# Another order of work in three stages of a fused attention and feed-forward kernel: GpSimd in the experts, all engines in the latent attention, the last units of the feed-forward

## The reference

```python
x = x + grouped_attention(layernorm(x), ctx, ctx)   # 32 query heads, 8 heads of ctx, width 8
x = x + routed_experts(layernorm(x))                # top 2 of 8 experts and 4 identities, SiLU gate
x = x + latent_attention(layernorm(x), ctx)         # 16 heads, rotary queries and keys
x = x + mx_feed_forward(layernorm(x))               # 256 -> 1024 -> 256, SiLU gate
# latent attention, per head h:
q   = rope(x @ Wq[h].T @ w_kc_q[h]) @ W_qr[h]       # 128x256 -> 192 -> 64
k   = rope(ctx) @ W_kr[h]
p   = softmax(q @ k.T)
out = sum_h (p @ rope(ctx)) @ w_kc_kv[h].T @ Wo[:, h].T
# feed-forward: inputs and weights are quantised in blocks of 32 (shared power of two, few mantissa bits)
```

## Time and profile before

| | us |
|---|---|
| median of 3 runs (lowest, highest) | 818.46 (818.2, 818.87) |
| the profiled execution | 819.62 |
| its span, first to last instruction | 817.80 |
| busy in the span: TensorE / VectorE / GpSimd / ScalarE | 749.2 / 594.5 / 567.1 / 403.1 |
| mean granted clock of TensorE | 0.981 of full |

### The profile page before, as it was taken

The page is one execution under the profiler, slowest core; times in us unless marked ns, Lnnn a source line. Parts: engine busy times, 40 slices in busy tenths (PEclk is TensorE's granted clock), DMA queues, the critical chain, the costliest instruction groups (busy, mean ns, idle before and its releaser), DMA issues. The chain is left out here.

```text
span 817.8 us, 14830 instructions
## 1 busy us (share of the span) xinstructions
PE 749.2 (92%) x4801; PEld 538.7 (66%) x4808; DVE 594.5 (73%) x1087; ACT 403.1 (49%) x1068; POOL 567.1 (69%) x590
## 2 busy tenths in 40 slices
PE   3999999878999998789999999999999999876786
PEld 2555555457888887656877777777777777653464
DVE  5888889856777878656465575886678675749994
ACT  1688887532323323226455545545444545454463
POOL 5677776425867667465656878787887787817996
PEclk9999999979999999989999999999999999997999
DMA  9300000040100010322200000000000000000001
GB/s 249 122 2 0 0 0 1 1 171 1 39 20 19 19 58 0 107 76 70 84 15 1 1 1 2 2 1 1 1 1 1 2 1 1 1 2 7 26 34 39
DMA packets 8763, 24.12 MB, mean 29 GB/s; under 512 B 1711, under 2 KB 5167, under 8 KB 8087
## 3 DMA queue, kind: packets, MB, share of 16 engines
q1 hardware_dynamic: 8154, 23.28, 8.6%
q10 hardware_dynamic: 549, 0.08, 0.1%
HBM read 21.26 MB, written 2.10 MB: 29 GB/s over the span
## 5 line engine op out<-in xcount | busy, mean ns | idle before, releaser
L1622 POOL TENSOR_TENSOR q<-turned 64x512 f32<-64x512 f32 x128 | 168.0, 1312 | 25.7 <-DVE turned L1548 9.5
L1299 PE MATMUL ps<-l_yt,a 128*128 128x512 f32 x576 | 146.0, 404 | 2.1 <-ACT p L1445 1.7
L1299 PEld LDWEIGHTS ps<-l_yt,a 128*128 128x128 f32 x576 | 106.2, 190 | 27.8 <-issue 4.7
L1609 POOL TENSOR_TENSOR p<-p,l_inverse 128x512 f32<-128x512 f32 x64 | 66.9, 1047 | 74.7 <-DVE l_inverse L1570 74.3
L1445 ACT ACTIVATE p<-ps,l_negmax 128x128 f32<-128x128 f32 x256 | 91.1, 382 | 43.2 <-DVE l_negmax L1539 43.1
L1548 DVE TENSOR_TENSOR turned<-ps,rope 128x1024 f32<-128x1024 f32 x64 | 78.1, 1221 | 45.0 <-PE ps L1299 42.3
L881 PE MATMUL ps<-yt_experts,wsplit 128*128 (+1 forms) x384 | 97.1, 401 | 0.2 <-DVE inner L979 0.2
L467 DVE TENSOR_REDUCE negmax<-ps 128x4 f32<-128x512 f32 x128 | 85.2, 686 | 14.8 <-PE ps L290 13.4
L881 PEld LDWEIGHTS ps<-yt_experts,wsplit 128*128 128x128 f32 x384 | 71.1, 192 | 14.4 <-DVE inner L979 0.5
L1539 DVE TENSOR_REDUCE l_negmax<-ps 128x4 f32<-128x512 f32 x64 | 41.2, 686 | 44.3 <-PE ps L1357 44.1
L383 ACT ACTIVATE pt<-ps 128x512 f32<-128x512 f32 x128 | 69.9, 599 | 5.2 <-PE ps L312 3.5
(11 more groups left out here) (214 smaller groups left out, 1566.5 us busy)
## 6 DMA issues: line engine op xcount, KB each, us to landing
wide<-in_wide SPq DMA_DIRECT2D x8, 768.0 KB, 4.4
mx_raw<-in_mx SPq DMA_DIRECT2D x8, 384.0 KB, 3.1
x<-in_x SPq DMA_DIRECT2D x4, 512.0 KB, 9.1
ctx_t<-in_ctx_t SPq DMA_DIRECT2D x1, 2048.0 KB, 7.9
out<-x SPq DMA_DIRECT2D x16, 128.0 KB, 1.7
narrow<-in_narrow SPq DMA_DIRECT2D x8, 192.0 KB, 2.8
ktraw<-in_ctx_rows SPq DMA_DIRECT2D x1, 1248.0 KB
wraw<-in_gate SPq DMA_DIRECT2D x1, 1024.0 KB, 18.8
```

The lines of the kernel that those rows point to most:

```text
L1299: out = pe.matmul(tile_bank(n, k), a[i][:, pa, kin, k * 128:(k + 1) * 128], yt[j % 2][:, py, kin, :, :].rearrange("p b s -> p (b s)"), sta ...
L1609: pool.tensor_tensor(p[:, head, :, :], p[:, head, :, :], spread(inverse[:, head, :], 2, S), ALU.mult).then_inc(normed[head], 1)
L1622: t = pool.tensor_tensor(out[rows[(head + half) % 2], head, :], turned[rows[head], half, :], turned[rows[head], 2 + half, :], ALU.add)
```

## The change

Experts: in a step GpSimd now does `ht`, divide, rotate, scale, quantise (the quantising moves behind rotation and scaling), and `scale_x` moves from x = 6 and 7 to 5 and 6. The memset of the bound is one more step of the semaphore chain of the routes (21 becomes 22).

Latent attention: TensorE's list becomes tiles 0 and 1, spare 0, tile 2, narrow product of n-1, spare 1, context of n-3, scores of n-1, both heads' transposes of n-2, spare 2, both halves of the projection of n-3, spare 3. The narrow product's full matmul is split into two of 64 columns, one per head. The context moves to bank 1, p's transposes to another of the changing banks and to the bank of the narrow product, and the waits follow the banks. The places `spare` hold query weights half 0, context weights, query weights half 1, narrow weights; the next group's rows are transposed at places 0 and 2, front's result at 2. ScalarE's copy of the context moves behind `qs`, VectorE's low part of it behind the rotations, and front's pieces on VectorE move from the end of its list to between the maxima and the first rotation, at k = 3, 4, 6, 7, 8, 9 (`deviations` at 4). SyncE also waits for the query weights before it loads the next wide weights.

Feed-forward: the multiplication by the scale of unit 14, and of the second half of unit 15, move from GpSimd to VectorE, behind the clips, with a semaphore `late_made`.

```diff
@@ routed_experts, GpSimd
-                if x == 6:
+                if x == 5:
                     pool.tensor_tensor(group, group, run_of(factor[:, :, :], j).to_broadcast([S, 4, E]),
...
                 if inside(u - 3, UNITS):
                     pool.wait_ge(h_hi, u - 2)
                     pool.tensor_tensor(ht[old][:, 1, :], h[old][:, :], ht[old][:, 0, :].bitcast(F32),
                                        ALU.subtract).then_inc(h_lo, 1)
+                if inside(v, UNITS) and x % 2 == 0:
+                    divide(4 * jv + xv // 2, xv)
                 if inside(u, UNITS) and x < ROTARY_STEPS:
                     rotate_context(pool, m, rotated, j, x)
-                if inside(u, UNITS) and x in (6, 7):
+                if inside(u, UNITS) and x in (5, 6):
                     scale_x(j, x)
+                if inside(v, UNITS) and x % 2:
+                    quantise(4 * jv + xv // 2, xv)
@@ latent_attention
-        ctx_ps, rows_ps = q_ps, m.ps16[:, 1, :]
+        ctx_ps, rows_ps = m.bank(1), m.ps16[:, 1, :]
...
-        turned_p_bank = lambda n, head: (changing[n % 2], m.bank(3))[head]
+        turned_p_bank = lambda n, head: (changing[(n + 1) % 2], q_ps)[head]
@@ latent_attention, SyncE
                 wait(sp, c_made, i - 1)
+                wait(sp, a_made, 2 * (i - 1))
                 load_wide(sp, m, d, i)
@@ latent_attention, TensorE: narrow_product
-                    wait(pe, cs_lo, n - 1)
+                    wait(pe, p_kept[1], n - 1)
...
-                    pe.matmul(q_ps, b[i][:, 1, :], q[n % 2][:, 2, :], start=False, stop=True).then_inc(narrowed, 1)
+                    for head in range(2):
+                        t = pe.matmul(q_ps[rows[head], :], b[i][:, 1, head * CE:(head + 1) * CE], q[n % 2][:, 2, :],
+                                      start=False, stop=True)
+                    t.then_inc(narrowed, 1)
@@ latent_attention, TensorE: context
                     wait(pe, cs_lo, n)
+                    pe.wait_ge(tile_turned, min(TILES * (n + 3) + 2, TILES * STEPS))
@@ latent_attention, TensorE: the list of a step
                 tile(n, 2)
                 narrow_product(n - 1)
                 spare(n, 1)
+                context(n - 3)
+                score(n - 1)
                 turn_p(n - 2, 0)
+                turn_p(n - 2, 1)
+                spare(n, 2)
                 project(n - 3, 0)
-                turn_p(n - 2, 1)
                 project(n - 3, 1)
-                spare(n, 2)
-                score(n - 1)
-                context(n - 2)
                 spare(n, 3)
@@ latent_attention, ScalarE: the list of a step
                 exponential(n - 2, 0)
-                keep_context(n - 3)
                 exponential(n - 2, 1)
                 spare(n, 0)
                 keep_narrow(n - 1)
                 spare(n, 1)
+                keep_context(n - 3)
                 keep_p(n - 2, 0)
                 keep_p(n - 2, 1)
@@ latent_attention, VectorE: the list of a step
                 maximum(n - 2, 0)
                 maximum(n - 2, 1)
+                for k, part in ((3, f.add), (4, f.statistics), (6, f.scales), (7, f.divide), (8, f.clip), (9, f.multiply)):
+                    if front_in(n, k) is not None:
+                        part(dve, m, front_in(n, k))
                 rotate_both(n, 0)
                 invert(n - 2, 0)
-                split_context(n - 3)
                 rotate_both(n, 1)
                 invert(n - 2, 1)
                 spare(n, 0)
                 rotate_last(n)
                 spare(n, 1)
+                split_context(n - 3)
                 spare(n, 2)
...
-                for k, part in ((2, f.add), (3, f.statistics), (6, f.scales), (7, f.divide), (8, f.clip), (8, f.multiply)):
-                    if front_in(n, k) is not None:
-                        part(dve, m, front_in(n, k))
@@ feed_forward, VectorE
                 if n == B:
+                    scale_back(n - 2)
                     clip_halves()
+                    scale_back_half()
...
+            def scale_back(n):
+
+                wait(dve, hq_turned, n - 1)
+                dve.wait_ge(hc_made, n + 1)
+                dve.tensor_tensor(blocks(hq[n % 2][:, :]), blocks(hc[n % 2][:, :]), spread(hscale[n % 4][:, :], 2, MX),
+                                  ALU.mult).then_inc(late_made, 1)
+
+            def scale_back_half():
+
+                dve.wait_ge(hq_turned, B - 2)
+                dve.wait_ge(hc_made, B + 1)
+                dve.tensor_tensor(half_of(hq[1], 1), half_of(hc[1], 1), spread(hscale[(B - 1) % 4][:, 16:32], 2, MX),
+                                  ALU.mult).then_inc(late_made, 1)
```

More of the change, by code:

```diff
@@ L44 @@
 TOP_SCALE = 1.5
-ROUTE_STEPS, ROTARY_STEPS = 21, 5
+ROUTE_STEPS, ROTARY_STEPS = 22, 5
 HEADS, CQ, CQH, KDIM = 16, 192, 96, 128
@@ L1083, in step @@
                     pool.wait_ge(rotated, ROTARY_STEPS * j + x)
-                if inside(u, UNITS) and x == 7:
+                if inside(u, UNITS) and x == 6:
                     pool.wait_ge(affine, j + 4)
@@ L1276, in spare @@
                         pe.wait_ge(y_lo, 2 * j + 1)
-                    turn(j, place, w_ps)
-                if fj is not None and place == 0:
+                    turn(j, place // 2, w_ps)
+                if fj is not None and place == 2:
                     pe.wait_ge(y_lo, 2 * min(fj + 2, GROUPS - 1) + 2)
@@ L1423, in spare @@
                         keep_narrow_weights(i, w_ps)
-                if j is not None and place < 2:
-                    keep_rows(j, place, w_ps)
-                if fj is not None and place == 0:
+                if j is not None and place in (0, 2):
+                    keep_rows(j, place // 2, w_ps)
+                if fj is not None and place == 2:
                     f.keep(act, fj, rows_ps)
@@ L1518, in spare @@
                 if i is not None:
-                    if place < 2:
-                        split_queries_weights(i, place, w_ps)
-                    elif place == 2:
+                    if place in (0, 2):
+                        split_queries_weights(i, place // 2, w_ps)
+                    else:
                         split_context_weights(i, w_ps)
-                if j is not None and place < 2:
-                    split_rows(j, place, w_ps)
+                if j is not None and place in (0, 2):
+                    split_rows(j, place // 2, w_ps)
             def last_statistics():
@@ L2009, in body @@
                     wait(pool, hq_turned, n - 2)
-                    for half in range(2):
-                        pool.wait_ge(hc_made, B + half)
-                        pool.tensor_tensor(half_of(hq[1], half), half_of(hc[1], half),
-                                           spread(hscale[(place - 1) % 4][:, half * 16:(half + 1) * 16], 2, MX),
-                                           ALU.mult).then_inc(hq_made, 1)
-                elif inside(n - 1, B):
+                    pool.wait_ge(hc_made, B)
+                    pool.tensor_tensor(half_of(hq[1], 0), half_of(hc[1], 0), spread(hscale[(B - 1) % 4][:, 0:16], 2, MX),
+                                       ALU.mult).then_inc(hq_made, 1)
+                elif inside(n - 1, B - 2):
                     pool.wait_ge(hc_made, n)
```

73 lines of the change are left out of this document (40 added, 33 removed).

## The result

The changed kernel took 805.65 us (median of 4 runs, 802.32 to 809.57) beside 818.33 of the kernel before (4 runs, 817.68 to 818.87): ratio 0.9847, interval 0.9802 to 0.9892, that is 12.7 us less where 12.5 were forecast. Run again (experiment `after_again`), it took 807.14 beside 819.18: 0.9837, interval 0.9816 to 0.9858. So the sum came out. That it came out this near is in part luck: of its terms some were too large and some too small by 1 to 2 us, and these errors cancel; the part on why lists them.

What follows compares the result with a forecast made beforehand. TensorE bounds the latent attention, GpSimd and VectorE waits the feed-forward, GpSimd's `ht` the experts' holes. -9.1 - 1.5 - 1.4 + 4.0 - 3.8 - 0.7 = -12.5 us, from 818.46 to 806.0 us, range 800 to 814.5.

Steps and rivals of the forecast that it cites:

- the order in steps 7 to 30: Latent attention, TensorE: two fewer tile changes at 0.19 us save 0.38 a step, -9.1 us in all (-4.3 to -10.6).
- the waits: Latent attention: copies, normalisations, turned rows and front's pieces arriving late in the new step cost +4.0 us together.
- steps 3 to 6: Latent steps that also make the weights: they lose at least as many tile changes, -1.5 us.
- the tail: Last latent iterations: the last scores stand behind one context instead of two transpose and project blocks, -1.4 us (-2.4 to 0).
- steps 0 to 2: First three latent steps: they wait for VectorE's splits of the weights either way, 0 us (-1 to +4).
- the experts: GpSimd's rotation ahead of quantising closes three TensorE holes, -2.85 us; scalings one place earlier, -1.0; together -3.8.
- the feed-forward's end: Unit 14's multiplication and the last second half move from GpSimd to VectorE: -0.7 us, between -0.2 and -1.5.
- rival 2: Latent blocks: tile changes are not what makes them long, so the overheads stay; 816.6 us, chance 0.08.
- The normalisations: ScalarE's later work delays the third tile in steps 9, 13, 21 and 29 by 0.3 us each.
- rival 1: Latent steps: waits for `qs` (+5.6 us), or pieces on VectorE and ScalarE, eat most of the gain; 810 to 814.5, chance 0.22.
- rival 3: Narrow product: the second pair of halves doesn't run side by side, +30.7 us, 837 us; chance 0.05.
- Front's pieces: VectorE, ahead of the rotations: `scales` in steps 14, 22 and 30 delays them, +0.3 us each, +0.9; at worst +5.

Runs made afterwards that it cites:

- experts_only: The kernel before with the experts' part of the change alone: 816.83 us, ratio 0.9968.
- unsplit: The changed kernel with the narrow product's second part in one piece of 128 columns again, the order kept: 817.32 us, ratio to the kernel before 0.9973.
- turns_together: The kernel before with the second head's four transposes moved ahead of both halves of the projection, nothing else: 821.3 us, ratio 1.0036.
- front_late: The changed kernel with front's pieces on VectorE behind the last split of a step again, at their old steps: 815.14 us, ratio to the kernel before 0.9958.
- split_alone: The kernel before with only the narrow product's second part split into two halves, the order kept: 819.55 us, ratio 1.0003.
- scale_late: The changed kernel with GpSimd's two scalings of x back in steps 6 and 7 of a group: 806.06 us, ratio to the kernel before 0.9831.
- ff_only: The kernel before with the feed-forward end of the change alone: 817.61 us, ratio 0.9971.
- latent_only: The kernel before with the latent part of the change alone: 810.88 us, ratio 0.9884.

## Why the prediction was right, step by step

Against the forecast, the order in steps 7 to 30 saved 1.8 us more, the waits cost 1.2 less and steps 3 to 6 saved 0.5 more; the tail came out 1.5 worse, steps 0 to 2 0.7, the experts 0.3 and the feed-forward's end 0.2. Each is taken up below.

**The change of tile: its price right, the whole gain a little too small.** Forecast 0.38 a step, found 0.45 (10.873 - 10.420), in 24 steps 10.9 us instead of 9.1, 0.3 beyond the upper bound; against the 10.85 of `experts_only` it is 10.4. The two changes themselves are 0.36 (`unsplit`), 0.18 each where 0.19 was taken; rival 2 is out. The other 0.07 to 0.09 is there with five changes too: 0.02 to 0.04 of it comes with the transposes in one block (`turns_together`), and the rest may lie in which tiles meet; that was not isolated. The upper bound itself was added up wrongly: 0.27 + 0.17 are the shares of two blocks and not of two changes. With the projection's 0.08, which the working puts to the same change as the scores' 0.27, the two largest changes make 0.52, or 12.5 us. I also looked for the overhead mostly in the block behind the change. The first halves, 1.01 or 0.91 by what follows them, show that the block ahead of a change carries part of it. So the context, with no change ahead of it any more, did not fall under 0.95, as I had named for a sign, but only to 0.97; a change still stands behind it. The tiles, whose share I could not separate, gave 0.11. The Trainium skill (TensorEngine Tiling (Array Packing), "Key Properties") states that changing the tiling mode, not merely the tile, drains TensorE. These runs agree as far as they go: a change of mode takes 0.18 to 0.24 us here at full clock. That it is a drain, they do not show.

**The waits, forecast +4.0, found +2.8** (256.47 - 264.60 + 10.9). The rows of the next group: 1.16 above a plain step (1.23 in step 7) and 0.1 in the step behind it, before 0.88 (0.85), so about +0.4 in three steps; 0.35 was forecast. The normalisations: +0.19 in steps 10, 14, 22 and 30 where 0.3 was taken; `f.keep` with it in step 17: +0.58 in step 18, where 0.8 was taken. This is the hole of 0.3 before step 18's third tile:

```profile
549.64 1.66 PE L1311 MATMUL ps<-l_yt,a 128*128 128x512 f32 x6 [0.30 <-ACT p L1463]
```

In steps 10 and 14, where I had named a hole of 0.3 as a sign, no idle time shows; the matmul only starts late. The scores' wait for `qs` found its 0.2 (0.16), so rival 1 did not come; rival 3 is out with 1.77 for all eight passes.

**Front's pieces: the term is nothing, and the price of leaving them was not seen.** I took +0.9 for `scales`, which does hold up the first rotation of step 14 (its four passes run from 504.19 to 506.23, the rotation begins at 506.27, 3.5 into the step), but the context didn't come to wait. What I left out is the old place: with the context ahead of the scores and the maxima at the end of the step, the pieces of before would have cost 9.6 us (`front_late`; steps 14, 22 and 30 are the same with and without the move). The move is a condition of the new order, not an extra; I priced what it added and not what it prevented.

**The tail: forecast -1.4, found +0.1.** The step that failed is that it ends with the scores. They did come earlier, 2.74 us behind the narrow product (701.35 - 698.61) instead of 4.37 (717.96 - 713.60): -1.6. TensorE and ScalarE before, from the last narrow product on:

```profile
713.60 1.08 PE L1313 MATMUL ps<-q,b 128*64 128x512 f32 x4 [2.73 <-POOL q L1627]
717.96 1.20 PE L1357 MATMUL ps<-keys,qs 64*128 64x128 f32 x16
719.88 0.37 ACT L1445 ACTIVATE p<-ps,l_negmax 128x128 f32<-128x128 f32 x1 [1.93 <-DVE l_negmax L1539]
722.77 0.66 PE L1324 MATMUL ps<-ident,p 128*128 128x128 f32 x4 [2.03 <-POOL p L1609]
725.95 1.13 PE L1370 MATMUL ps<-l_pt,kvr 128*64 128x128 f32 x16
```

The changed kernel:

```profile
698.61 1.08 PE L1325 MATMUL ps<-q,b 128*64 128x512 f32 x4 [3.18 <-POOL q L1645]
701.35 1.16 PE L1374 MATMUL ps<-keys,qs 64*128 64x128 f32 x16
703.13 1.09 ACT L1487 ACTIVATE l_pt<-ps 128x512 f32<-128x512 f32 x2 [1.07 <-PE ps L1341]
704.11 0.37 ACT L1463 ACTIVATE p<-ps,l_negmax 128x128 f32<-128x128 f32 x1
707.00 0.66 PE L1341 MATMUL ps<-ident,p 128*128 128x128 f32 x4 [1.01 <-POOL p L1627]
710.91 1.09 PE L1388 MATMUL ps<-l_pt,kvr 128*64 128x128 f32 x16
```

The two copies of turned `p` of the step before now stand ahead of the last exponentials, which begin 2.76 behind the scores' start instead of 1.92: +0.8. And the last context stands behind both heads' transposes and the whole projection, 3.91 behind the first of these transposes (710.91 - 707.00) instead of 3.18: +0.7. With 0.2 more ahead of the narrow product the gain is spent. Both tails ran at full clock; with low-clock stretches in it the tail of the changed order takes up to 34.15 (`after_again`).

**Steps 0 to 6.** Steps 3 to 6 gained 2.0 where 1.5 was taken; 0.50 a step, near the 0.45 of the later ones. Steps 0 to 2, put at 0, have become longer. They can be compared only between profiles with the same time at low clock in them: with 6.83 us of it the old order takes 38.64 to 38.71 (`before`, `split_alone`, `turns_together`, `experts_only`) and the new 39.35 to 39.40 (`after`, `scale_late`, `front_late`), with 3.41 us the old 37.62 (`ff_only`) and the new 38.31 and 38.40 (`latent_only`, `after_again`). That is +0.7 either way; where it comes from was not looked into.

**Experts, -3.8 forecast, -3.5 found.** The three holes gave 2.7 and the last 0.9, as worked out. The reason given for the last was wrong: it is not the scalings' earlier place but the quantising behind them (`scale_late`).

**Feed-forward, -0.7 forecast, -0.65 found**, for the multiplication took 1.85 on VectorE, nearer to the f_yq rows than to the clip. At full clock the part behind the last transposes is 0.2 longer, which the forecast left out, so the end as a whole gives about 0.5. The Trainium skill (SBUF — State Buffer, "Who interferes with whom") has such an instruction of VectorE wait for the whole of a GpSimd instruction that reads SBUF. This trace nearly agrees: tile f_yq of the changed kernel, the same multiplication (durations in ns, first and last start), has

```profile
L1765 DVE TENSOR_TENSOR f_yq<-f_yc,f_yscale x3: 1215/1636/1640, 534.6 to 703.9; 128x1024 bf16<-128x1024 bf16 x3
```

The one of 1215 starts at 703.9, when GpSimd has nothing to do; unit 14's, 1.85, starts 0.77 before GpSimd's second half of h8 ends (791.32) and ends 1.08 behind that end. A wait for the whole of it and then a pass of 1.215 would make 1.99, so the two overlap by some 0.1. The 0.2 to 0.5 that the prediction worked out by this rule holds for the end as a whole, not for the last transposes alone. The low-clock stretch of the old end was named as worth 1.5 us either way; it may be what the runs of `ff_only` gained beyond the 0.67 of the trace.

## What to carry to other kernels

Where TensorE is full, count how often the tile of its array changes in a loop and lay blocks of one tile next to each other, even at the price of a product in two halves. Change the order and split the product together: in steps 7 to 30 the split alone gave 1.0 to 1.4 us, the order without it nothing (265.04 beside 264.60), and both 8.1. When an order is turned round, price what the old place of every other piece would cost in the new order too, and follow the last iteration to the stage's end: here a gain forecast for the tail was spent again behind the scores. On an engine that waits once per unit, work that nobody waits for belongs ahead of the instruction that waits, not behind it.

## What the runs showed that I had not expected

The spread of the changed kernel's times, 802.3 to 809.6 us, goes with TensorE's clock: its first profile ran at 0.989 of full clock in mean, that of 807.41 at 0.983, with steps 7 to 30 the same to 0.02 us. The old order's steps 7 to 30 repeat to 0.4 us (264.21 to 264.60 in three profiles). So a saving of 1 us can be read from a stage of a trace of such a kernel, not from a few of its times.

In the old feed-forward end the clock fell to 1.2 GHz for 3.41 us in three of five profiles, in the new end in none of seven. Ahead of its last transposes TensorE had waited four times for about 1 us (1.11, 1.11, 0.93 and 1.12, in 802.45 to 810.08); in the new end the wait of 0.93 is gone, and only three are left (1.11, 1.11, 1.25). That this is the cause is not shown, and two profiles speak against it as it stands: the ends of `split_alone` and `turns_together` have the same four waits (1.11, 1.11, 0.92 or 0.93, 1.12 or 1.11), and their clock did not fall.
